# Delta attention on one core: ScalarE takes the roots before the queries' activation, and the last output projection is cut in two around the last turned outputs

## The reference

```
q = silu(x @ Wq.T);  k = silu(x @ Wk.T);  v = x @ Wv.T;  beta = 2 * sigmoid(x @ Wbeta.T)
k = k * rsqrt(sum(k * k, per head) + EPS)
o = delta_rule(q, k, v, beta)           # S += k (beta (v - k S)); o = q S, over 512 tokens
gate = sigmoid(x @ Wg1.T @ Wg2.T);  og = o * gate
og = og * rsqrt(mean(og * og, per head) + EPS) * g_norm
return og @ Wo.T
x = layernorm(x + that)
```

## Time and profile before

| | |
|---|---|
| median of 3 runs | 3053.31 us (3050.89 to 3059.13) |
| profiled execution | 3055.48 us, span 3053.7 us |
| PE busy | 2623.9 us (86%) |
| DVE busy | 1903.3 us (62%) |
| ACT busy | 1459.2 us (48%) |
| POOL busy | 1147.6 us (38%) |
| mean granted clock of TensorE | 0.923 of full speed |
| stage 1 (delta) | 0 to about 697 us of the span |
| stage 2 (scan) | about 697 to 1238 us |

### The profile page before, as it was taken

The page is one execution under the profiler, slowest core; times in us unless marked ns, Lnnn a source line. Parts: engine busy times, 40 slices in busy tenths (PEclk is TensorE's granted clock), DMA queues, the critical chain, the costliest instruction groups (busy, mean ns, idle before and its releaser), DMA issues.

```text
span 3053.7 us, 50551 instructions
## 1 busy us (share of the span) xinstructions
PE 2623.9 (86%) x20138; PEld 1427.1 (47%) x20154; DVE 1903.3 (62%) x2978; ACT 1459.2 (48%) x2605; POOL 1147.6 (38%) x1072
## 2 busy tenths in 40 slices
PE   7889999886887866899989898988769999999787
PEld 5666666552332322688644454544433333333244
DVE  4343343437999999566265656657646666677377
ACT  4342424226656664234263553626316666666355
POOL 0545454515877776000153426162232333331000
PEclk9899999897988988999989999899879999999899
DMA  3323131412304140323333323244165445442301
GB/s 94 91 63 91 55 100 53 106 43 103 132 1 145 40 141 14 152 85 121 128 115 111 101 84 93 98 135 143 36 143 117 104 106 116 105 110 52 127 28 42
DMA packets 196766, 284.50 MB, mean 93 GB/s; under 512 B 84388, under 2 KB 86468, under 8 KB 195636
## 3 DMA queue, kind: packets, MB, share of 16 engines
q1 hardware_dynamic: 196532, 281.27, 31.6%
HBM read 192.08 MB, written 63.31 MB: 84 GB/s over the span
## 4 chain that ended last, share of the span: by engine, by line
PE 41%; DVE 10%; issue 4%; ACT 4%; POOL 2%; DMA 2%; SPq 1%; DVEq 0%; ACTq 0%; POOLq 0%
PE ps L236 8%; PE ps L3625 4%; PE ps L3638 4%; PE ps L2065 4%; PE ps L2076 4%; PE ps L3557 3%; PE ps L3574 2%; PE ps L3608 2%; PE ps L2731 1%; PE ps L3562 1%; DVE arena L2994 1%; PE ps L2739 1%; DMA arena<-arena 1%; DVE arena L1669 1%; DVE arena L2992 1%
## 5 line engine op out<-in xcount | busy, mean ns | idle before, releaser
L236 PE MATMUL ps<-arena 128*128 128x512 f32 (+3 forms) x1280 | 471.7, 521 | 15.2 <-ACT arena L2831 6.1
L3810 DVE TENSOR_REDUCE cross<-ps 128x1 f32<-128x512 f32 x512 | 327.5, 685 | 175.8 <-PE ps L3608 175.7
L3718 ACT ACTIVATE cross<-ps 128x512 f32<-128x512 f32 x512 | 276.6, 592 | 156.0 <-PE ps L3625 155.5
L1701 POOL TENSOR_TENSOR arena<-arena 128x1024 f32<-128x1024 f32 x128 | 305.9, 2393 | 119.6 <-DVE arena L1693 119.4
L236 PEld LDWEIGHTS ps<-arena 128*128 128x128 f32 (+2 forms) x1296 | 193.9, 155 | 245.5 <-issue 174.1
L1717 PE MATMUL ps<-arena 128*128 128x512 f32 x512 | 268.9, 667 | 37.9 <-POOL arena L1701 37.6
L1693 DVE TENSOR_TENSOR_SCAN arena<-ps,arena 128x1024 f32<-128x1024 f32 x128 | 291.4, 2277 | 9.4 <-ACT ps L1684 9.3
L1684 ACT ACTIVATE ps<-arena 128x511 f32<-128x511 f32 x256 | 165.1, 679 | 158.1 <-DVE arena L1693 157.9
L609 POOL TENSOR_TENSOR arena<-arena 128x31 f32<-128x31 f32 (+15 forms) x217 | 133.0, 613 | 223.3 <-DMA arena<-d_a 206.9
L1717 PEld LDWEIGHTS ps<-arena 128*128 128x128 f32 x512 | 105.5, 214 | 192.2 <-issue 125.0
L3625 PE MATMUL ps<-cross,cross 50*128 50x512 f32 x512 | 156.0, 503 | 32.5 <-ACT cross L3718 22.8
(11 more groups left out here) (360 smaller groups left out, 5138.2 us busy)
## 6 DMA issues: line engine op xcount, KB each, us to landing
arena<-d_bc SPq DMA_DIRECT2D x32, 1024.0 KB, 5.4
cross<-d_parts SPq DMA_DIRECT2D x192, 128.0 KB, 4.6
arena<-d_x SPq DMA_DIRECT2D x16, 1024.0 KB, 5.3
d_parts<-cross SPq DMA_DIRECT2D x32, 512.0 KB, 3.5
d_x<-arena SPq DMA_DIRECT2D x48, 256.0 KB, 2.5
arena<-in_D_wlm SPq DMA_DIRECT2D x12, 1024.0 KB, 6.2
d_signs<-arena SPq DMA_DIRECT2D x32, 256.0 KB, 2.1
arena<-arena SPq DMA_DIRECT2D x64, 128.0 KB, 2.1
```

The source lines that it names most:

```text
L236: ins = pe.e.matmul(ps[:m, :n], lhsT(k), rhs(k), start=(k == 0), stop=(k == chunks - 1))
L1701: pool.e.tensor_tensor(h, h, s.bc[turn % s.SLOTS][:, 1], ALU.mult).then_inc(*pool.up("scan_hC"))
L3718: act.e.activation(s.E[:, k % 2, j], s.rexp.bank((u, i)), ACT.Exp).then_inc(*s.rexp.empty(act, (u, i)))
L3810: dve.e.tensor_reduce(s.mx[:, u % 2, t, h:h + 1], s.rmax.bank((u, m)), AX.X, ALU.max, negate=True).then_inc(*s.rmax.empty(dve, (u, m)))
```

## The change

In `act_all` the call of `act_queries` in the even turns moves behind the two square roots. In turn 8, `pe_all` no longer does OT and then the whole of y: it does the first two chunks of all four tiles of y (`pe_out_first`), OT, and the other two chunks (`pe_out_rest`). The ring's order stays the same. The line numbers of the changed kernel are 4 higher behind the first hunks, up to `pe_out`, 20 higher from `pe_keys` on, and 18 to 20 higher in `act_all`.

```diff
@@ pe_all
+            if p == s.PAIRS:
+                s.pe_out_first(pe, B - 1)
             if p >= 1 and p % 2 == 0:
                 s.pe_og(pe, p - 1)
             if front:
                 s.pe_keys(pe, n)
-            if p >= 1 and p % 2 == 0:
+            if p == s.PAIRS:
+                s.pe_out_rest(pe, B - 1)
+            elif p >= 1 and p % 2 == 0:
                 s.pe_out(pe, p // 2 - 1, 0)
...
-            if p >= 1 and p % 2 == 0:
+            if front and p >= 1 and p % 2 == 0:
                 s.pe_out(pe, p // 2 - 1, 1)
...
+    def pe_out_first(self, pe, b):
+        s, R = self, self.ring
+        pe.e.wait_ge(*R.at_emptied(pe, ("OT", 2 * b, 1)))
+        for t in range(T):
+            pe.e.wait_ge(*R.at_free(pe, ("y", b, t)))
+            for k in range(s.E):
+                pe.e.matmul(R.bank(("y", b, t)), s.ogT[:, k, t * P:(t + 1) * P], s.wo[:, k, :], start=(k == 0), stop=False)
+
+    def pe_out_rest(self, pe, b):
+        s, R = self, self.ring
+        pe.e.wait_ge(*R.at_emptied(pe, ("OT", 2 * b + 1, 1)))
+        for t in range(T):
+            for k in range(s.E, C):
+                ins = pe.e.matmul(R.bank(("y", b, t)), s.ogT[:, k, t * P:(t + 1) * P], s.wo[:, k, :], start=False, stop=(k == C - 1))
+            ins.then_inc(*R.fill(pe, ("y", b, t)))
@@ act_all
-            if front and p % 2 == 0:
-                s.act_queries(act, n)
             if p >= 1:
                 act.e.wait_ge(*act.on("delta_og_squares", p - 1))
                 act.e.activation(s.oss, s.oss, ACT.Sqrt).then_inc(*act.up("delta_og_root"))
...
+            if front and p % 2 == 0:
+                s.act_queries(act, n)
             if back and p % 2:
                 s.act_triangles(act, p)
```

## The result

The changed kernel takes 3032.18 us (median of four runs, 3027.68 to 3035.68) where the kernel before, run beside it, takes 3056.22 (four runs, 3050.89 to 3060.29). The ratio is 0.9916, with a 95% interval from 0.9900 to 0.9931. The forecast was 3025.1 us in a range from 3015 to 3042, against a time before of 3053.3. Two later comparisons of the same kernel gave 0.9906 [0.9886, 0.9926] and 0.9888 [0.9865, 0.9911]. Taken on the time before, the three are gains of 25.7, 28.7 and 34.2 us, and the forecast was 28.2.

What follows compares the result with a forecast made beforehand. The prediction took TensorE's idle time to bound the delta stage and VectorE's in-order work the scan stage; gains of 20.7 and 7.5 us, 28.2 together, took 3053.3 to 3025.1 us, range 3015 to 3042.

Steps and rivals of the forecast that it cites:

- What bounds the kernel: Delta stage: TensorE's idle time counts; scan stage: an in-order train of VectorE work that starts when delta ends.
- Part 1: Boundaries 2, 4 and 6: roots ahead of the queries' Silu remove TensorE's idle time and low clock; gain 20.7 us.
- The open term: Boundary 2: VectorE's scaling of the outputs lasts 2.56 us with GpSimd running beside it, 1.22 us with GpSimd idle.
- The table loads: ScalarE: seven added loads of 1.28 us, 9.0 us together, lie in idle time, with no drain beside them.
- Boundary 0: First boundary: roots first gain nothing, since VectorE is still at the first inversion; price 0.
- Part 2: End of delta: half of the last projection runs ahead of the turned outputs, in TensorE's wait; gain 7.5 us.
- The sum: Whole kernel: 20.7 + 7.5 = 28.2 us gained, from 3053.3 to 3025.1 us.
- The rival of a fixed price of the order: Chains of pairs 2, 4, 6, from the experiments: new order costs the same 6 us each run; no chance given.
- A: Boundaries and end: idle time goes but TensorE's clock stays low; gain 23.0 us, 3030; forecast with this 70%.
- B: Delta stage: only the last projection's split counts, something else holds the turned outputs or y; 3039 to 3046 us; 15%.
- C: Start of scan: gain given back to transfers or ScalarE's work; 0 to 9 us stay, 3044 to 3053; 10%.
- D: Scan stage: shifted phases against TensorE's clock make it slower; with 25 groups 14 us slower, 3068; 5%.

Runs made afterwards that it cites:

- warm_gap: Kernel before plus six unused 128x512 matmuls filling TensorE's wait at boundaries 2, 4 and 6; 3047.77 us against 3054.91, ratio 0.9972.
- extra_switch: Changed kernel plus two useless ScalarE activations, forcing two more table loads, at boundaries 2, 4 and 6; 3039.32 us in one run.
- split_only: Kernel before with only the last projection split in halves around the turned outputs, queries' Silu still ahead of the roots; 3048.47 us, ratio 0.9971.
- sums_inside: Changed kernel with boundary 0's keys' squares and scaling moved into VectorE's first inversion, at steps 22 and 24; 3022.36 us in one run.
- tile3_between: Changed kernel with tile 3's part of y's first half moved behind the turned outputs; 3026.80 us in one run.
- roots_only: Kernel before with only ScalarE's two roots moved ahead of the queries' Silu, last projection left whole; 3037.05 us against 3058.35, ratio 0.9922.
- before_again: Kernel before, run again without an edit; 3056.11 us in one run.
- after_again: Changed kernel, run again without an edit; 3028.65 us, ratio 0.9906 to the kernel before.
- after_third: Changed kernel, run a third time without an edit; 3023.85 us, ratio 0.9888 to the kernel before.
- both_more: Changed kernel with the edits of tile3_between and sums_inside together; 3024.12 us against 3057.45 for the kernel before, ratio 0.9896.

## Why the prediction was right, and the size that was off

**What bounds the kernel.** Right. The delta stage is bound by TensorE and its waits; 23.5 us taken out there came out as 22.5 in the span, and the second stretch is 0.9 us longer. One reading was loose: the scan stage ends at 1238, and the second window of the earlier trace rows runs to 1340. Up to 1238 VectorE is busy 510.29 of 541.00 us, which bears the same reading out.

**Part 1, 20.7 us.** Right in mechanism; 22.3 measured, a little above the upper end of 21.6. The queries' end to the end of y's first half at boundary 2 is 231.31 - 222.33 = 8.98 us, for which I had 9.5. I let y start 2.4 us after the queries; it starts 1.85 after them, because the 16 transposes take 1.9 us (2.2 in the sum) and the multiplications of the turned outputs run beside the keys' transposes, so that y follows these after 0.1 us. The open term, the scaling's duration, came out at its lower end: 1.23 us. The idle time and the clock behind it both went, as forecast, and warm_gap shows them apart.

The rule of the Trainium skill's "SBUF — State Buffer", section "SBUF: two separate sides", was put to a harder test than I had thought. GpSimd's short step L609 (128x60) started 0.18 us behind the scaling and took 1.29 us. The same step before:

```profile
220.13 0.38 POOL L609 TENSOR_TENSOR arena<-arena 128x60 f32<-128x60 f32 x1
```

The two exclude each other, and the later one waits: VectorE at boundary 2 before (2.56 us), GpSimd now. The trace agrees with the rule. The next two steps of GpSimd took 1.38 and 1.11 us for 0.31 and 0.25, beside two more VectorE operations of 128x1024. For these three GpSimd's transfer goes out 2.9 us later (224.58 against 221.66), and nothing at this boundary waits for that.

**The table loads.** Right for after: seven more loads, no wait from them. The row decides against the drain of the Trainium skill's "ScalarE: Activation LUTs", "What ACT_TABLE_LOAD costs": the load at 218.09 begins 0.02 us behind the activation before it, and the root at 219.38 starts 0.01 us behind its end. The margin of the queries' load is thinner than "hidden by the queries" sounds: extra_switch shows that 3.0 us more on ScalarE cost 2.45 at the boundary.

**Boundary 0.** Price 0 forecast; 16.3 us before, 16.1, 16.4 and 16.3 in the three profiles of after.

**Part 2, 7.5 us.** Right: 7.6 measured, and 16.09 in split_only alone. OT comes 1.6 us behind the end of the scaling (1.8 forecast), and the second half of y starts 1.96 us behind OT's start (1.95 forecast).

**What failed.** The sum took the time between the boundaries as unchanged. That term was set at 0 and came out at 6.4 us lost in this profile. The parts in it are not of one kind. The 1.74 us of pair 6 are a slower way of GpSimd's inverse through memory, which did not come again in the two other profiles. The 3.44 us of pair 2 and the 1.86 of pair 4 go with TensorE's clock: over the eleven profiles without warm_gap's (60.22 us with 10.2), pair 2's chain takes 61.9 to 62.5 us with 10.2 us at the lower clock, 64.0 to 64.6 with 13.6 or 13.7, and 65.5 to 65.9 with 17.0 or 17.1. Pair 4 shows it over all twelve, warm_gap among them:

| pair 4: us at the lower clock | length of the chain, us | profiles |
|---|---|---|
| 0.0 | 56.7, 57.0 | sums_inside, before |
| 3.4 | 57.5, 57.6 | tile3_between, roots_only |
| 6.8 | 58.8, 58.8, 59.1 | after, split_only, before_again |
| 10.2 | 60.2, 60.2, 60.4 | after_again, after_third, warm_gap |
| 13.7 | 61.8, 62.1 | both_more, extra_switch |

The rival of a fixed price of the order falls, since roots_only and tile3_between run the same instructions up to pair 6 and lose only half of it in pair 2, and sums_inside, with the roots first as well, has 62.48. An edit elsewhere, or only another run of before, moves this chain by 2 to 3 us. So the 6.4 us belong to this pair of profiles: between the two profiles of before and the three of after, the last residual moved by 23.5 to 27.0 us.

**The rivals of the prediction.** A falls by the 1.04 us of OT at every boundary. B falls by roots_only, whose 24 us are more than the whole of it. C and D fall by the second stretch, which has the length and the clock of before (2359.2 us for 2358.3; in the two other profiles of the changed kernel it lasts 2356.7 and 2360.2).

**What stays open.** The same chain of pair 2 came out at 65.80, 65.88 and 65.77 us in three profiles of the changed kernel, and at 64.0 and 64.2 in two kernels with the same order there. So the place of the stretches at the lower clock looks fixed by the kernel there, though the two profiles of before differ by 2.2 us (62.36 and 64.55). I can't say what in the kernel fixes it. Nor can I say whether roots that stand first make long ones more likely: the chains of pairs 2, 4 and 6 together take 178.9 to 179.2 us in the three profiles of after and 172.1 and 176.4 in the two of before, but 172.8 to 176.6 in four other kernels with the roots first (extra_switch, with its two added switches, has 180.7). In time the three comparisons spread from 25.7 to 34.2 us, with 29.5 as their mean. The forecast of 28.2 lies among them, but its closeness is in part luck: part 1 came out 1.6 us above its term, and the stretches between, set at 0, took back 1.1 to 6.4 us, by which of the two profiles of before and the three of after are set side by side.

## What to carry to other kernels

When an engine waits for a very short operation, look at what stands ahead of that operation on its own engine: an in-order queue can make it wait for a long result that it doesn't need. A switch of ScalarE's table (1.28 us here) was free only where the engine had that much to spare in front of a wait of its own, so read that slack first. And price a closed gap twice, once for its idle time and once for TensorE's clock behind it, but leave some microseconds open for what the clock does in stretches that were not touched.

## What the runs showed of the hardware that was not expected

- A table load can run ahead of its activation's wait. At boundary 2 the load for L300 ran at 229.74, and the activation it is for waited until 242.44. It doesn't always: at 187.93 the load in front of L1069 came only after 5.15 us of idle time, and its activation followed at once. What decides between the two, no run here tests.
- A VectorE multiplication of 128x1024 and GpSimd's elementwise steps exclude each other to the price of whichever starts second: 1.29 instead of 0.38 us for a step of 128x60 now, 2.56 instead of 1.22 for the multiplication in the kernel before, beside a step of 1.89 us.
- TensorE can be given the lower clock while it is busy without a gap of note: in after it is busy 8.24 of 8.24 us from 281.30 at a granted clock of 1.00, then 8.22 of 8.22 at 0.82, and then 7.71 of 8.23 at 0.56. In pair 4, over twelve profiles, the chain went from 57 us with none of it at the lower clock to 62 us with 13.7.
- Eight transposes of 128x128 in fp32 take 1.04 to 1.09 us at a granted clock of 1.00 and 1.97 at 0.50.
